# A new order for the front of a fused attention and feed-forward kernel

## The reference

```python
# x: (8, 1024, 512); per 128-row segment, 8 heads of 64, segments in sequence
q, k, v = xs @ Wq, xs @ Wk, xs @ Wv
sq, sk = elu(q) + 1, elu(k) + 1
att_mem = sq @ mem / (sq @ z)                 # memory of the earlier segments
mem, z  = mem + sk.T @ v, z + sk.sum(rows)
att_dot = softmax(q @ k.T * scale) @ v
att = gate * att_mem + (1 - gate) * att_dot   # gate = sigmoid(betas)
x = layernorm(x + att @ Wo)
W1q, W2q = quantize(W1), quantize(W2)         # clip(round(W / (mean|W| + 1e-5)), -1, 1)
x = layernorm(x + relu(x @ W1q.T + b1) @ W2q.T + b2)
```

## Time and profile before

| | before |
|---|---|
| median of 3 runs | 1899.68 us (1899.41 to 1900.86) |
| the profiled execution | 1899.23 us, its span 1897.3 us |
| PE busy | 1851.0 us, 98% of the span |
| DVE, ACT, POOL busy | 76%, 53%, 40% |
| mean granted PE clock | 0.992 |

### The profile page before, as it was taken

The page is one execution under the profiler, slowest core; times in us unless marked ns, Lnnn a source line. Parts: engine busy times, 40 slices in busy tenths (PEclk is TensorE's granted clock), DMA queues, the critical chain, the costliest instruction groups (busy, mean ns, idle before and its releaser), DMA issues.

```text
span 1897.3 us, 44351 instructions
## 1 busy us (share of the span) xinstructions
PE 1851.0 (98%) x16447; PEld 1307.6 (69%) x16447; DVE 1447.7 (76%) x2935; ACT 1002.5 (53%) x2422; POOL 765.9 (40%) x775
## 2 busy tenths in 40 slices
PE   5789999999999999999999999999999999999998
PEld 3566677766677766677766677766677766677765
DVE  7777777787877787777787877777777777777774
ACT  5755544545555545555545555545555545555541
POOL 1214345444345444335444344444344444344443
PEclk9899999999999999999999999999999999999999
DMA  8412433323333323333323333323333323333110
GB/s 272 124 25 47 63 58 64 65 39 60 63 59 62 62 43 60 63 58 63 67 39 60 64 59 61 68 38 60 60 63 60 69 41 56 60 59 63 35 24 23
DMA packets 556420, 117.47 MB, mean 62 GB/s; under 512 B 529824, under 2 KB 533808, under 8 KB 555696
## 3 DMA queue, kind: packets, MB, share of 16 engines
q1 hardware_dynamic: 556208, 114.64, 31.4%
HBM read 50.54 MB, written 16.80 MB: 35 GB/s over the span
## 4 chain that ended last, share of the span: by engine, by line
PE 93%; DVE 4%; ACT 2%; issue 1%; DMA 0%; POOLq 0%; SPq 0%; DVEq 0%; POOL 0%; ACTq 0%
PE bank L427 12%; PE bank L426 12%; PE bank L440 12%; PE bank L441 11%; PE bank L276 6%; PE bank L278 6%; PE bank L277 6%; PE bank L364 3%; PE bank L409 3%; PE bank L408 3%; PE bank L407 3%; PE bank L290 3%; PE bank L343 3%; PE bank L291 3%; PE bank L292 3%; PE bank L395 2%
## 5 line engine op out<-in xcount | busy, mean ns | idle before, releaser
L426 PE MATMUL bank<-yt,w1t 128*128 128x256 f16 x2048 | 453.9, 273 | 0.2 <-DVE yt L802 0.2
L427 PE MATMUL bank<-yt,w1t 128*128 128x256 f16 x2048 | 453.9, 273 | 0.0
L1145 ACT ACTIVATE prob<-bank,exp_bias,gscalars 128x128 f32<-128x128 f32 x512 | 227.6, 454 | 363.6 <-DVE exp_bias L719 358.6
L440 PE MATMUL bank<-w2t,arena 128*128 128x512 f16 x1024 | 388.4, 379 | 0.0
L441 PE MATMUL bank<-w2t,arena 128*128 128x512 f16 x1024 | 388.1, 379 | 0.0
L1189 ACT ACTIVATE arena<-bank,b_scaled,wscalars 128x256 f32<-128x256 f32 x512 | 263.1, 570 | 207.9 <-PE bank L427 155.0
L854 DVE CAST arena<-arena 128x512 f16<-128x512 f32 x256 | 153.8, 601 | 93.2 <-ACT arena L1189 92.5
L1312 POOL TENSOR_TENSOR att_mem<-att_mem,gate_in 128x512 f32<-128x512 f32 x60 | 87.1, 1452 | 330.9 <-DVE att_mem L758 319.9
L426 PEld LDWEIGHTS bank<-yt,w1t 128*128 128x128 f16 x2048 | 200.4, 98 | 23.5 <-issue 0.6
L427 PEld LDWEIGHTS bank<-yt,w1t 128*128 128x128 f16 x2048 | 200.3, 98 | 22.8
L1390 POOL TENSOR_TENSOR arena<-arena 128x512 f16<-128x512 f32 x128 | 155.2, 1213 | 86.9 <-DVE arena L854 86.9
(11 more groups left out here) (186 smaller groups left out, 4300.4 us busy)
## 6 DMA issues: line engine op xcount, KB each, us to landing
rows<-in_L_attn_x SPq DMA_DIRECT2D x32, 512.0 KB, 3.8
out_rows<-rows SPq DMA_DIRECT2D x64, 256.0 KB, 2.3
x_blocks<-in_L_attn_x SPq DMA_DIRECT2D x248, 64.0 KB, 3.0
sk<-sk_t SPq DMA_DIRECT2D x480, 32.0 KB, 2.0
att_dot<-att_mem SPq DMA_DIRECT2D x480, 32.0 KB, 2.0
y_blocks<-rows SPq DMA_DIRECT2D x480, 32.0 KB
arena<-in_L_ffn_W SPq DMA_DIRECT2D x6, 1024.0 KB, 5.4
w2t<-in_L_ffn_W SPq DMA_DIRECT2D x2, 1024.0 KB, 13.1
```

The source lines that it names most:

```text
L426: pe.matmul(ps[:, c], w1t[:, k, cols], yt[:, g % 2, :, k], start=k == 0, stop=False)
L427: ins = pe.matmul(ps[:, c], w1t[:, k, cols], yt[:, g % 2, :, KT + k], start=False, stop=k == KT - 1)
L440: pe.matmul(banks[own][:], h_hi[:, f, toks], w2t[:, f, :], start=f == 0, stop=False)
L1145: ins = act.activation(prob[:, t, at], ps[:, c], ACT.Exp, scale=gcol(g, G_EXP), bias=exp_bias[:, t, at:at + 1], accum_out=row_sum[:, t, h: ...
```

## The change

Only the order inside rounds 0 and 1 (and a few clips in round 2) is written anew, with the waits that this needs:

- The scales of q and v are made in one chain (`CHAINS = ("k", "qv", "o")`): three chains in place of four.
- In round 0, `project_v` comes ahead of `scores`, the o weight's maximum comes after both halves of the first `score_max`, and its hi split on ACT goes behind `xt_hi(1, 1)`.
- All 32 turns of the feed-forward weights stand in round 1: groups of four behind each of the four k and q projections, four behind `project_v`, and the rest behind `scores(1, 1)`, `turn_y(0, 0)` and `attend(1, 0)`. Blocks from 16 on cycle over four banks (0, 1, 6, 7).
- The threshold for W1 and its first three roundings stand at the end of DVE's round 0, behind `mem_add(0, 0)`; that for W2 stands in round 1.
- The feed-forward scale (`ffn_scale`) is cut into three helpers.
- `ffn_up(0, 0)` waits for 29 of the 32 puts, and for the four clips of W1.

```diff
+        CHAINS = ("k", "qv", "o")
+        def w_bank(n):
+            return n % 2 if n < 16 else (0, 1, 6, 7)[n % 4]
# turn_w (PE)
-                if n >= 2:
+                if 2 <= n < 18:
                     pe.wait_ge(sem["wput"], n - 1)
+                elif n >= 20:
+                    pe.wait_ge(sem["wput"], n - 3)
# ffn_up (PE)
-                    pe.wait_ge(sem["clipped"], NBLOCKS // 4)
+                    pe.wait_ge(sem["clipped"], 4)
+                    pe.wait_ge(sem["wput"], NBLOCKS - 3 + n)
# PE, round loop
                 update_memory(g - 1, 1)
                 if g == 1:
-                    for n in range(20, 24):
-                        turn_w(n)
+                    sum_all(1)
                 project_qk(g, "k", 0)
...
                 if g == 1:
-                    for n in range(24, 28):
+                    for n in range(0, 4):
                         turn_w(n)
...
                 if g == 0:
+                    project_v(g, 0)
+                    project_v(g, 1)
                 scores(g, 0)
...
                 turn_y(g - 1, 1)
                 ffn_down(g - 2, 1, 3)
-                if g == 0:
-                    for n in range(4, 8):
-                        turn_w(n)
-                    sum_all(2)
                 attend(g, 0)
                 read_memory(g, 1)
                 if g == 0:
-                    for n in range(8, 12):
-                        turn_w(n)
-                    for n in range(12, 16):
+                    spread_bias_max()
+                if g == 1:
+                    for n in range(28, 32):
                         turn_w(n)
                 attend(g, 1)
# DVE, end of round 0 (mem_add(0, 0) and scalars(1, ..) stand ahead)
+                if g == 0:
+                    ffn_scale()
+                    threshold(1)
+                    round_w(0)
+                    round_w(1)
+                    round_w(2)
# ACT
                 xt_hi(g + 1, 0)
                 if g == 0:
-                    for n in range(12, 16):
+                    xt_hi(1, 1)
+                    w_split("o", 0)
+                    w_split("o", 1)
+                    w_sum(2, 0)
```

More of the change, by code:

```diff
@@ L513, in _ @@
                 if g == 1:
+                    sum_all(1)
+                project_qk(g, "k", 0)
+                if g == 0:
+                    turn_max(1)
+                    turn_bias()
+                    spread_max(1)
+                ffn_up(g - 2, 5)
+                if g == 1:
+                    for n in range(0, 4):
+                        turn_w(n)
+                else:
+                    turn_att(g - 1, 0)
+                project_qk(g, "k", 1)
+                if g == 1:
+                    for n in range(4, 8):
+                        turn_w(n)
+                    turn_att(0, 0)
@@ new lines, in _ @@
+                project_qk(g, "q", 0)
+                ffn_up(g - 2, 6)
+                if g == 1:
+                    for n in range(8, 12):
+                        turn_w(n)
+                project_qk(g, "q", 1)
+                if g == 1:
+                    for n in range(12, 16):
+                        turn_w(n)
+                turn_att(g - 1, 1)
+                if g == 1:
+                    sum_all(2)
+                ffn_up(g - 2, 7)
+                project_out(g - 1, 0)
+                project_out(g - 1, 1)
@@ new lines, in _ @@
+                if g == 0:
+                    project_v(g, 0)
+                    project_v(g, 1)
+                scores(g, 0)
+                if g:
+                    project_v(g, 0)
+                    ffn_down(g - 2, 0, 0)
+                    project_v(g, 1)
+                if g == 0:
+                    turn_max(2)
+                if g == 1:
+                    for n in range(16, 20):
+                        turn_w(n)
+                turn_p(g, 0, 0)
+                ffn_down(g - 2, 0, 1)
@@ L514, in _ @@
+                if g == 0:
+                    spread_max(2)
+                ffn_down(g - 2, 0, 2)
+                scores(g, 1)
+                if g == 1:
                     for n in range(20, 24):
                         turn_w(n)
-                project_qk(g, "k", 0)
+                read_memory(g, 0)
+                ffn_down(g - 2, 0, 3)
+                ffn_down(g - 2, 1, 0)
+                ffn_down(g - 2, 1, 1)
+                turn_p(g, 0, 1)
                 if g == 0:
-                    turn_max(2)
@@ L951, in _ @@
             w_max("k")
[L952 to L953 removed]
+            w_chain(0)
+            w_scale(0)
             xt_lo(0, 0)
@@ L1226, in _ @@
             for g in range(NG + 2):
+                h_relu(g - 2, 4)
+                qk_split(g, "k", 0)
                 if g == 0:
-                    w_sum(1, 1)
-                h_relu(g - 2, 4)
+                    w_split("v", 0)
+                    w_split("v", 1)
+                if g == 1:
+                    for n in range(0, 4):
+                        put_w(n)
+                qk_split(g, "k", 1)
+                h_relu(g - 2, 5)
+                if g == 1:
+                    for n in range(4, 8):
+                        put_w(n)
+                    w_sum(2, 1)
+                at_hi(g - 1, 0)
+                qk_split(g, "q", 0)
+                if g == 0:
+                    gates()
+                if g == 1:
+                    for n in range(8, 12):
+                        put_w(n)
+                else:
+                    at_hi(g - 1, 1)
+                h_relu(g - 2, 6)
+                qk_split(g, "q", 1)
+                if g == 1:
+                    for n in range(12, 16):
+                        put_w(n)
+                    at_hi(0, 1)
+                if g == 0:
+                    v_split(g, 0)
+                    v_split(g, 1)
+                    w_sum(1, 3)
+                h_relu(g - 2, 7)
+                exponentials(g, 0, 0)
+                if g:
+                    v_split(g, 0)
+                exponentials(g, 0, 1)
+                if g == 0:
+                    w_sum(1, 0)
+                p_split(g, 0, 0)
+                if g:
+                    v_split(g, 1)
+                if g == 1:
+                    for n in range(16, 20):
+                        put_w(n)
+                exponentials(g, 1, 0)
+                exponentials(g, 1, 1)
+                p_split(g, 0, 1)
+                p_split(g, 1, 0)
                 if g == 1:
```

301 lines of the change are left out of this document (107 added, 194 removed).

## The result

| | before | changed |
|---|---|---|
| median | 1899.78 us (1899.41 to 1900.86, 4 runs) | 1926.91 us (1924.24 to 1927.53, 4 runs) |
| profiled execution, span | 1899.23, 1897.3 us | 1926.73, 1924.7 us |
| PE busy | 1851.0 us, 98% | 1849.4 us, 96% |
| `update_memory(0, 0)` starts | 79.25 us | 84.79 us |
| `ffn_up(0, 0)` starts | 125.74 us | 150.93 us |

The account below looks back on a forecast made before the run. PE was taken as the bound, so only the start of `ffn_up(0, 0)` counts: update at 87 us plus 66.5 gives 153.5, 27.8 us later, so 1927.5 us. Own range 1920 to 1935; stated range 1912 to 1936 us.

Parts of the forecast that it names:

- Only the product's start can change the time: PE is busy without waits from 130 us on, so any shift of `ffn_up(0, 0)` reaches the end in full; 27.8 us later.
- PE waiting after 160 us: Sign of a wrong forecast: the late front shifted something else too, first the copies of x for group 2.
- Step 1: DVE up to group 0's scalars: done at 24.0 us instead of 27.87, as joining the q and v chains saves 3.9 us.
- Step 2: DVE from group 0's scalars to group 1's x scale: 30.2 us of work plus 6.5 of waits, ending at 60.7 us.
- the lower bound by the bounce: Earliest x scale of group 1 that the maxima's trip out to DRAM and back allows: 59 us.
- Steps 3 to 5: ACT's first o hi half at 63.0 us, POOL's halves done at 73.2, SP's sk copies landed and update at 87.
- The path: From update to `ffn_up(0, 0)`: 46.5 before, 13 for 20 more turns, thresholds 3 and 2, clock 2; 66.5 us.
- the two thresholds: New PE waits between update and feed-forward: about 3 us for W1 behind the update, 2 us for W2 before the output projection.
- The clock term: After a 25 us hole, the update and k's projection run partly at the lower PE clock: 2 us, paid once.
- Rival (a): Turns lie wholly in round 1's gaps, PE works without pause from the update: 53.3 us to the product, 1914 us; chance 0.12.
- Rival (b): PE's clock falls where turns and puts alternate, all four projections take 4.5 us: 5.7 us more, 1933 us; chance 0.08.
- Rival (c): The sk copies do not hold up the update, feed-forward starts at 121.6 us: 1895.5 us, not slower; chance 0.04.

Follow-up runs that it names:

- e1: Changed kernel with ACT making the o weight's hi half behind group 0's first p split, not behind group 1's x; ratio 1.0076 to the kernel before.
- e2: Changed kernel with SP issuing the 16 sk copies ahead of the transfer that waits for POOL and of the gates' return; ratio 1.0058 to the kernel before.
- e7: Kernel before with only the scales of q and v joined in one chain, all else in the old order; ratio 0.9999.
- e11: e10 with all 32 turns cycling over four banks (0, 1, 6, 7); ratio 1.0009 to the kernel before.
- e12: e11 with turn_att(0, 1) and at_hi(0, 1) ahead of blocks 12 to 15's turns and puts, and block 15 in bank 0; ratio 0.9990 to the kernel before.
- e4: Changed kernel with all 32 turns cycling over four banks, not only those from block 16 on; ratio 1.0128 to the kernel before.
- e10: e9 with e1's edit, the o weight's hi half made early on ACT; ratio 1.0025 to the kernel before.
- e3: Changed kernel with the feed-forward scale, W1 threshold and first three roundings ahead of DVE's first memory addition; ratio 1.0140 to the kernel before.
- e5: Changed kernel with the edits of e2, e3 and e4 together; ratio 1.0048 to the kernel before.
- e8: Changed kernel with the edits of e2 and e3, and six sk copies issued ahead of the maxima's way back on SP; ratio 1.0050 to the kernel before.
- e9: e8 with SP's two gate transfers ahead of feed-forward part (2, 1) instead of behind it; ratio 1.0026 to the kernel before.

## Why the prediction was right, step by step

- **Only the product's start can change the time.** Right for the size, not to the last 2 us: product +25.2, span +27.4. The product was forecast at 153.5 us and came at 150.93, 2.6 us earlier; the late loss of 2.2 us, which the prediction put at nothing, made up for it. So the mechanism was right, but that the forecast came within 1 us of the measured time is luck. At 700 us one of SP's 16 copies of y took long to issue; the columns are the shortest, median and longest issue in ns, and the starts of the first and last:

```profile
L1537 SPq DMA_DIRECT2D y_blocks<-rows x16: 598/611/4361, 700.8 to 714.3; - x16
```

  Behind them PE waited 1.1 us at 720.6 and 0.6 us at 730.8 us; 0.5 us at 661.4 us lie ahead of them. PE waiting after 160 us was on the prediction's list of signs of being wrong, with the copies of x for group 2 as the first suspect; the waits came, small, and the slow copies next to them are those of y. That these copies are the cause was not tested. The kernel before has such long issues too (16 copies of y in 12.77 us at 674.77 us, for 10.41 at 731.52), on copies with time to spare. Why they come, and why they hit these copies in the changed kernel, e1 and e2, was not tried.
- **Step 1**, scalars at 24.0 us: 23.94. Right, and e7 shows that by itself this step is worth nothing.
- **Step 2**, x scale at 60.7 us: 58.64. DVE's work was right (30.1 us for 30.2), its waits were too high in my walk (4.6 us for 6.5); the bounce was issued at 45.12 and came back from 52.21 us, so the lower bound by the bounce (59) was nearer.
- **Steps 3 to 5**: the first half of `wo_hi` ready at 61.16 us (63.0), POOL's end at 71.42 (73.2), and 13.4 us from there to the update (13.7). So the update's 2.2 us come from step 2. e1 and e2 each cut this chain at another link and take 14.2 and 17.8 us off the update.
- **The path**, 66.5 us: 66.14. The sum was right, its terms less so. The turns took 18.16 us of PE in the stretch instead of 7.08, and 11.7 us of waits where the kernel before had 0.9. The turns' line alone:

```profile
84.79:151.30 66.51, 18.16 (x128) 13.81 (x128) 0.94 0.25 65
```

  PE's idle time in the stretch went from 7.98 to 16.59 us. Of the 8.6 us, 3.6 are the two thresholds (forecast 5), so 5.0 are the turns' waits less old gaps that they fill. With 11.1 us of work this is 0.80 us for each of 20 blocks, not 0.65, and above the 0.72 us that the prediction took as its upper price: 16.1 us instead of 13. The clock term of 2 us was seen at its place (update 2.00 us for 1.15, k's projection 4.3 for 2.6), but the kernel before had paid as much elsewhere in its stretch: 0.93 then, 0.94 now. Its net is near zero. (The two levels that the prediction read from the lengths of products are there again: products of 128x256 take 0.42 us until 92.4 us, in a stretch (84.79 to 93.00 us) with a granted clock of 0.52, and 0.27 us behind it. In 20.43 to 24.95 us of the kernel before the profile gives 1.00, though most of the products take 0.42 us, so there the lengths say more than the column.) The errors of +3.1, -1.4 and -2.1 us leave 0.4 us; that they cancel so nearly is luck.
- **Rival (a)**, work without a pause: excluded by the waits of 11.7 us. e11 and e12 came to 61.1 and 59.9 us, not to 53.3.
- **Rival (b)**, the clock falls in the alternating stretch: not in the changed kernel (1.00 from 93 to 151 us). But it is near: in e4 the clock was 0.51 around a pause of 4.13 us, in e12 it was 0.66 from 110 to 120 us with no pause over 2.2 us there. In the changed kernel and in e10 the same pauses of 1.6 to 2.2 us left it at 1.00. Which pauses cost clock was not settled.
- **Rival (c)**, the copies are no obstacle: excluded. Its condition, `wo_hi` before 49 us, was also too weak: it goes with the path of 53.3 us of rival (a). In e1 ACT began `wo_hi` at 45.1 us, PE still waited 9.4 us for the copies, and the product came 11 us later than in the kernel before. With a path of 66 us the copies would have to land before about 59 us. To come level took five edits together (e11: early `wo_hi`, copies ahead, early gates, early W1 threshold, four banks); how many of them could be left out was not tried.

## What to carry to other kernels

When work moves on one engine, follow its result through the queues of the engines whose lists stay as they are: here two instructions on ACT reached PE by way of POOL and one waiting transfer on SP, with sixteen urgent copies queued behind it. An order in such a queue has its reason in the other lists: the same SP edit brought the update 18 us forward in the new order and put it back by 7 us in the old. And when a hole closes, expect the next one close behind it: after the copies it was the gates and the thresholds. And split a stretch into work and idle time before you call a saving lost: the four banks had won their 5 us, and a lower clock behind them took it.

## What the runs showed of the hardware

- DVE's roundings and POOL's lo half slow each other: 2.12 and 2.85 us became 2.97 and 4.04 on POOL, and two roundings took 4.70 us for 2.48 on DVE (e3, and the same within 0.02 us in e5, e8, e9). With POOL's `att_mem` beside them it was 4.33 us for 2.48 on POOL and 3.50 for 2.48 on DVE (e10).
- One SP issue of a 32 KB copy of y takes 0.61 us in the median and now and then far longer: up to 3.96 us in the kernel before, 4.36 in the changed one, 4.77 in e1. Long ones are spread over the run (in the kernel before 3.6 us between 788 and 1480 us, 3.9 us after 1696 us).
- Nearly the same row of pauses left the granted clock at 1.00 in one kernel (changed, e10) and took it down in another (0.83 in 120 to 130 us in e8, 0.66 in 110 to 120 us in e12). A row of 16 transposes (four blocks) behind a pause of 2.15 us took 2.39 us in the first and 3.3 to 3.7 us in the second.
- The same 25.45 us of PE work from the W2 threshold to the feed-forward product took 31.02 us at a mean granted clock of 0.83 (e4) and 28.39 us at 0.90 (e11), with the same idle time of 6.6 us.
